# Values and denominators of a pair of steps in one column-tiled batch: 20 batches a group in place of 36

## The chip, the cores and the metric

One core of one Trainium2 chip runs the whole program in one launch. The metric is the device time of that launch in microseconds (us), lower is better. Durations come from one profiled execution; its own device time stands beside its span below.

## What is computed

One block of a language model over 2 x 2048 tokens of width 1024: an embedding of four-token contexts, layer norm, causal attention with 32 query heads over 8 key/value heads of width 32, its output projection, layer norm, and a last linear layer whose weight is corrected through a Fourier matrix. The change touches attention alone:

```
scores = jnp.einsum('bhqd,bhkd->bhqk', q, k) / math.sqrt(HEAD_DIM)
scores = jnp.where(causal[None, None, :, :], scores, jnp.float32(-1e+20))
attn = jax.nn.softmax(scores, axis=-1)
out = jnp.einsum('bhqk,bhkd->bhqd', attn, v)
```

## The kernel before

Three parts follow one another. `part_a` gathers the embeddings, normalises them and computes rotated queries, keys and values. `part_b` is attention. `part_c` is the output projection and the last layer. `part_b` takes most of the time and is all that changes.

**Groups and steps.** `part_b` runs 16 groups, each of one key/value head and its 4 query heads. A group has 36 steps (`STEPS`): for each of 8 query blocks `c` of 256 rows, first the diagonal block of 256 keys, then the `c` earlier ones. A step's work goes over four engines:

- PE computes the step's scores in two halves of 128 keys (`scores`, L1022). A half is two matmuls of 512 columns, into one of two slots of PSUM, `st_ps`. In a diagonal step each is followed by a small mask matmul (L1026). A half waits until the exponential of the same half of the step before has been taken (`exp_done`).
- ACT takes the exponential of each half (L878) into `probs`, which has 8 slots, one a step. Before it refills a slot it waits for PE and POOL to be done with it.
- POOL adds up the exponentials of a set of steps for the denominators (`set_sum`, L848 to L860). A set (`SETS`) is two steps, or the diagonal step alone where `c` is even: 16 pairs and 4 singles, 20 sets a group.
- PE multiplies by the values (`values`, L1040), three steps behind the scores (`LAG`), and with the last step of a set multiplies POOL's sum by ones (`denominators`, L1057, waits for `sum_done`). Both are column-tiled: the four heads are matmuls with 32 output columns each, which run side by side in the four quarters of the array. A step's values are 8 matmuls, which the profile shows as 16 records, the denominators 4, shown as 8. All else on PE uses the whole array.

**The maxima of the next rows.** Softmax needs each row's maximum before its scores. PE computes the scores of a later group once more in another layout (`row_scores`, L983, one matmul of 512 columns into one of three banks, `mx_ps`; the narrower blocks of the diagonal end with a mask matmul, L987), and DVE reduces each bank (L922). A bank is given again once DVE has reduced what it held (`max_done`). There are 140 such products and 4 transposes ("turn", L992) a group, four or five a step, 18 steps ahead of the scores (`LEAD`).

**The order of PE's work** is written out by hand in `group`: in each step two entries of the maxima, the two halves of the scores, two more entries (a fifth lies between the halves), then `batch(g, s - LAG)`.

Of the kernel before, what the change touches and what calls it, by code (L numbers as in the profile page):

```python
# [540 lines left out]
QW = CT // 2  # L541
# [11 lines left out]
LAG = 3  # L553
# [13 lines left out]

SETS = sum_sets()
SET_OF = [j for j, steps in enumerate(SETS) for s in steps]
LEAD, FIRST_LEAD = 18, 14  # L570
TURN_AFTER = 5
FOUR_AT, DELTA_AT = 8, 36
# [42 lines left out]
def part_b(nc, hand, w0_hi, w0_lo, q_hi, q_lo, k_hi, k_lo, v_dram, o_dram, den_dram, recip_dram, w_o_t, w_base_t,  # L615
           w1_dram, enc, fourier_t):

    with ExitStack() as ctx:
# [49 lines left out]
        def _(sp):  # L668
# [54 lines left out]
            def group(g, first, last):  # L723
                output_weight(g)
                first_reciprocals(g)

                def after_scores(s):
                    sp.wait_ge(st_ready, 2 * (g * NS + s + 1))

                def next_q(c):  # L730
                    if not last:
                        after_scores(LAST_OF_ROWS[c])
                        load_q(g + 1, c)
                    elif c < 2:
                        after_scores(LAST_OF_ROWS[c])
                        load_attended(sp, hand, o_dram, recip_dram, c)

                def next_k_max(c):
                    if not last:
                        sp.wait_ge(max_ready, g * NE + K_MAX_LAST[c] + 1)  # L740
                        load_k(k_max, g + 1, c, k_max_loaded)
                    elif c % 2 == 1:
                        sp.wait_ge(max_ready, g * NE + max(K_MAX_LAST[c - 1:c + 1]) + 1)
                        sp.dma_start(hand.w_in[c // 2][:], w1_dram[c // 2 * P:(c // 2 + 1) * P, :]
                                     ).then_inc(hand.w1_loaded[c // 2], 16)

                def next_k_score(c):
                    if not last:
                        after_scores(K_LAST[c])
                        load_k(k_score, g + 1, c, k_score_loaded)  # L750

                def next_v(c):
                    if not last:
                        sp.wait_ge(batch_done, g * NS + K_LAST[c] + 1)
                        load_v(g + 1, c)

                next_q(0)
                if not first:
                    store(g - 1, QH - 1)
                store(g, 0)  # L760
                send_rows(g, 2)
                next_k_max(0)
                store(g, 1)
                store(g, 2)
                next_q(1)
                next_k_max(1)
                store(g, 3)
                next_k_max(2)
                next_k_max(3)
                send_rows(g, 3)  # L770
                store(g, 4)
                next_q(2)
                if not last:
                    send_rows(g + 1, 0)
                store(g, 5)
                if not last:
                    send_rows(g + 1, 1)
                next_k_score(0)
                store(g, 6)
                next_k_score(1)  # L780
                next_v(0)
                next_k_score(2)
                next_v(1)
                next_q(3)
                next_k_score(3)
                next_v(2)
                next_v(3)

# [26 lines left out]
        @block.gpsimd  # L815
        def _(pool):
            nc.gpsimd.memset(k_score[M_ROW:P, :].bitcast(F32), 1.0).then_inc(k_ones_done, 1)
            pool.wait_ge(k_ones_done, 1)
            for c in range(DC):
                pool.wait_ge(base_in[c], 16)  # L820
                pool.wait_ge(delta_taken, c + 1)
                nc.gpsimd.tensor_tensor(hand.base[:, c, :], hand.base[:, c, :], hand.four[c][:], ALU.add
                                        ).then_inc(w1_ready, 1)

            for t in range(TPC):
                pool.wait_ge(hand.v_stored[t], 16 * CHUNKS)
            for s in range(2):
                pool.wait_ge(hand.rot_stored[s], 16 * CHUNKS * QK_TILES)
            step = Steps(pool, sum_step, 0)

            def probs_of(g, s, k, lo):
                return probs[:, (g * NS + s) % SLOTS, k, :, lo:QW]

            def exp_waited(g, s, k):
                pool.wait_ge(exp_done, 2 * (g * NS + s) + k + 1)

            def set_sum(g, j):

                q = g * len(SETS) + j
                at = sums[:, q % SUM_SLOTS]  # L840
                diagonal = [s for s in SETS[j] if STEPS[s][0] == STEPS[s][1]]
                wide = [(s, k) for s in SETS[j] for k in range(2) if k == 0 or s not in diagonal]
                if q >= SUM_SLOTS:
                    g_old, j_old = divmod(q - SUM_SLOTS, len(SETS))
                    pool.wait_ge(batch_done, g_old * NS + SETS[j_old][-1] + 1)
                if len(wide) == 1:
                    exp_waited(g, diagonal[0], 1)
                    nc.gpsimd.tensor_tensor(at[:, :, P:QW], probs_of(g, diagonal[0], 0, P),  # L848
                                            probs_of(g, diagonal[0], 1, P), ALU.add).then_inc(sum_done, 1)
                    return  # L850
                exp_waited(g, *wide[1])
                step.do(nc.gpsimd.tensor_tensor(at, probs_of(g, *wide[0], 0), probs_of(g, *wide[1], 0), ALU.add))  # L852
                exp_waited(g, *wide[2])
                step.do(nc.gpsimd.tensor_tensor(at, at, probs_of(g, *wide[2], 0), ALU.add))  # L854
                if diagonal:
                    lo, last = P, (diagonal[0], 1)
                else:
                    lo, last = 0, wide[3]
                exp_waited(g, *last)
                nc.gpsimd.tensor_tensor(at[:, :, lo:QW], at[:, :, lo:QW], probs_of(g, *last, lo), ALU.add  # L860
                                        ).then_inc(sum_done, 1)

            for g in range(GROUPS):
                for j in range(len(SETS)):
                    set_sum(g, j)

        @block.scalar
        def _(act):

            def exps(g, s, half):  # L870
                c, i = STEPS[s]
                n, lo = g * NS + s, P if i == c and half == 1 else 0
                act.wait_ge(st_ready, 2 * n + half + 1)
                if half == 0 and n >= SLOTS:
                    g_old, s_old = divmod(n - SLOTS, NS)
                    act.wait_ge(batch_done, n - SLOTS + 1)
                    act.wait_ge(sum_done, g_old * len(SETS) + SET_OF[s_old] + 1)
                nc.scalar.activation(probs[:, n % SLOTS, half, :, lo:QW], st_ps[:, half, :, lo:QW], ACT.Exp,  # L878
                                     scale=float(HD) ** -0.5).then_inc(exp_done, 1)

            def take(g, c):
                act.wait_ge(batch_done, g * NS + LAST_OF[c] + 1)
                if g * QH + c >= 2:
                    act.wait_ge(stored[c % 2], STORE * (g * (QH // 2) + c // 2))
                nc.scalar.copy(od_sb[:, c % 2], od_ps[:]).then_inc(od_copied, 1)  # L885
# [83 lines left out]
        def _(pe):  # L969
# [59 lines left out]
            def values(g, s):  # L1029
# [7 lines left out]
                for k in range(2):  # L1037
                    lo = P if i == c and k == 1 else 0
                    for h in range(GROUP):
                        mm = nc.tensor.matmul(od_ps[h * HD:(h + 1) * HD, 0, lo:QW], vs[:, 2 * i + k, :],  # L1040
                                              probs[:, n % SLOTS, k, h, lo:QW], start=s in FIRST_OF and k == 0,
                                              stop=False)
                return mm

            def denominators(g, s):

# [12 lines left out]
                return mm  # L1059

            def products(g, s):
                mm = values(g, s)
                if s == SETS[SET_OF[s]][-1]:
                    mm = denominators(g, s)
                mm.then_inc(batch_done, 1)

            def batch(g, s):
                if s >= 0:
                    products(g, s)
                elif g > 0:  # L1070
                    products(g - 1, s + NS)

            def group(g, first, last):
                for s in range(NS):
                    entries = entries_in(s, first, last)
                    ends = min(2, len(entries) // 2)
                    for more, n in entries[:ends]:
                        give(g + more, n)
                    scores(g, s, 0)
                    for more, n in entries[ends:len(entries) - ends]:  # L1080
                        give(g + more, n)
                    scores(g, s, 1)
                    for more, n in entries[len(entries) - ends:]:
                        give(g + more, n)
                    batch(g, s - LAG)

# [372 lines left out]
```

## Time and profile before

| | |
|---|---|
| median of 3 runs | 3505.76 us (3503.0 to 3506.37) |
| the profiled execution | 3505.48 us, span 3503.7 us |
| first to last column-tiled batch | 767 to 2752 us of the span |
| PE busy | 3364.4 us (96%) |
| DVE busy | 2239.2 us (64%) |
| ACT busy | 1420.5 us (41%) |
| POOL busy | 2265.2 us (65%) |
| TensorE clock granted | 0.982 of full speed |

PE is TensorE's matmul, PEld its weight load, which runs beside it. A matmul's record is longer than the distance to the next one's start, since they are pipelined. So what a matmul costs is read from start to start. "Idle before" names what ended the idle time of the engine.

### The profile page before, as it was taken

How to read it: one execution, taken by the hardware profiler on the slowest of the kernel's cores; microseconds unless marked ns; L12 is line 12 of the kernel's file. 1: busy time of each engine (PE TensorE's matmuls, PEld its weight loads, DVE VectorE, ACT ScalarE, POOL GpSimd, SP SyncE). 2: the span in 40 equal slices, each digit the busy share in tenths (PEclk: the TensorE clock that was granted, in tenths of full speed). 3: DMA queues.
4: the chain of work that ended last, by engine and by line, in shares of the span. 5: the costliest groups of instructions: out<-in, count | busy, mean ns of one | idle time of the engine just before them, and what ended most of it. 6: DMA issues, size and time to landing. Idle time of an engine off the chain costs nothing. (4 is left out here: it accounts for less than half of the span.)

```text
span 3503.7 us, 60330 instructions
## 1 busy us (share of the span) xinstructions
PE 3364.4 (96%) x24768; PEld 2343.2 (67%) x24768; DVE 2239.2 (64%) x3594; ACT 1420.5 (41%) x1677; POOL 2265.2 (65%) x1042
## 2 busy tenths in 40 slices
PE   1999999999999999999999999999999799999999
PEld 1778888646666666666666666666665488888887
DVE  3667777657777777777777777777774344444443
ACT  2222233125555555555555555555556300111100
POOL 3443320048999999999999999999999522333321
PEclk8999999969999999999999999999999899999999
DMA  8999984721221222122122112212212253344342
GB/s 231 245 255 232 234 226 127 193 101 41 65 61 34 63 63 56 38 66 58 40 68 60 41 49 64 51 39 67 55 39 52 85 99 94 91 95 93 87 95 67
DMA packets 248214, 334.52 MB, mean 95 GB/s; under 512 B 64346, under 2 KB 153818, under 8 KB 247938
## 3 DMA queue, kind: packets, MB, share of 16 engines
q1 hardware_dynamic: 229506, 263.54, 28.4%
q0 software_dynamic: 18432, 67.12, 9.0%
q8 instruction: 195, 3.19, 0.4%
q14 instruction: 81, 0.66, 0.1%
HBM read 227.80 MB, written 101.71 MB: 94 GB/s over the span
## 5 line engine op out<-in xcount | busy, mean ns | idle before, releaser
L922 DVE TENSOR_REDUCE mpart<-mx_ps 128x1 f32<-128x512 f32 (+3 forms) x2240 | 1407.3, 670 | 518.4 <-PE mx_ps L987 251.1
L878 ACT ACTIVATE probs<-st_ps 128x1024 f32<-128x1024 f32 (+1 forms) x1152 | 1063.0, 974 | 782.0 <-PE st_ps L1022 592.7
L983 PE MATMUL mx_ps<-k_max,qs 96*128 96x512 f32 (+3 forms) x2560 | 836.0, 410 | 4.3 <-PEq L158 2.6
L852 POOL TENSOR_TENSOR sums<-probs 128x1024 f32<-128x1024 f32 x256 | 610.3, 2384 | 119.7 <-ACT probs L878 119.7
L1022 PE MATMUL st_ps<-qs,k_score 98*128 98x512 f32 (+1 forms) x2304 | 676.9, 405 | 0.4
L854 POOL TENSOR_TENSOR sums<-sums,probs 128x1024 f32<-128x1024 f32 x256 | 614.4, 2400 | 20.6 <-ACT probs L878 0.6
L983 PEld LDWEIGHTS mx_ps<-k_max,qs 96*128 96x128 f32 x2560 | 444.3, 193 | 256.7 <-DVE mpart L922 148.2
L1040 PE MATMUL od_ps<-probs,vs 128*32 128x256 f32 (+1 forms) x9216 | 592.2, 375 | 0.4 <-ACT od_sb L885 0.4
L860 POOL TENSOR_TENSOR sums<-sums,probs 128x1024 f32<-128x1024 f32 (+1 forms) x256 | 539.3, 2107 | 20.5 <-ACT probs L878 0.5
L1022 PEld LDWEIGHTS st_ps<-qs,k_score 98*128 98x128 f32 x2304 | 431.2, 193 | 83.7 <-ACT probs L878 12.3
L1215 POOL TENSOR_TENSOR h<-h,bb 128x1024 f32<-128x1024 f32 x32 | 104.1, 3253 | 509.4 <-DVE xn_c L1289 509.4
L1040 PEld LDWEIGHTS od_ps<-probs,vs 128*32 128x32 f32 x9216 | 241.7, 109 | 259.0 <-issue 147.7
L291 POOL DMA_INDIRECT hbuf<-in_tok_table,idx_all x128 | 192.6, 1504 | 308.6 <-DMA hbuf<-in_tok_table,idx_all 168.3
L491 PE MATMUL qk_ps<-x_hi,w_hi 128*128 128x512 f32 x640 | 253.9, 397 | 18.3 <-ACT rotation L343 15.9
L491 PE MATMUL qk_ps<-x_lo,w_hi 128*128 128x512 f32 x640 | 251.0, 392 | 0.0
L491 PE MATMUL qk_ps<-x_hi,w_lo 128*128 128x512 f32 x640 | 251.0, 392 | 0.0
L1277 DVE TENSOR_TENSOR h<-oc_ps,h_in 128x1024 f32<-128x1024 f32 x31 | 38.0, 1224 | 256.3 <-PE oc_ps L1330 256.3
L1057 PE MATMUL od_ps<-sums,ones 128*32 128x256 f32 (+1 forms) x2560 | 184.5, 360 | 16.1 <-POOL sums L860 16.1
L987 PE MATMUL mx_ps<-masks 128*128 128x128 bf16 (+2 forms) x704 | 181.0, 257 | 0.0
L1242 ACT ACTIVATE std_c<-var_c 128x1 f32<-128x1 f32 x32 | 6.5, 203 | 404.2 <-DVE var_c L1284 404.2
L1330 PE MATMUL f_ps<-w_hi,xc_hi 128*128 128x512 f32 x512 | 158.6, 391 | 6.7 <-DVE xc_lo L1299 6.7
L1330 PE MATMUL oc_ps<-w_hi,a_hi 128*128 128x512 f32 x496 | 156.6, 397 | 7.5 <-DVE a_lo L1267 7.5
(108 smaller groups left out, 3950.1 us busy)
## 6 DMA issues: line engine op xcount, KB each, us to landing
qs<-q_hi_scratch SPq DMA_DIRECT2D x128, 256.0 KB, 4.8
h_scratch<-hbuf SPq DMA_DIRECT2D x32, 512.0 KB, 8.9
q_hi_scratch<-rot_hi SPq DMA_DIRECT2D x64, 256.0 KB, 4.1
q_lo_scratch<-rot_lo SPq DMA_DIRECT2D x64, 256.0 KB, 4.8
qs<-q_lo_scratch SPq DMA_DIRECT2D x64, 256.0 KB, 5.8
o_scratch<-od_sb SPq DMA_DIRECT2D x128, 128.0 KB
o_in<-o_scratch SPq DMA_DIRECT2D x32, 512.0 KB, 4.9
o_in<-recip_scratch SPq DMA_DIRECT2D x128, 128.0 KB, 7.9
```

The lines of the kernel that those rows point to most:

```text
L291: nc.gpsimd.indirect_dma_start(hbuf[:, m % 2, t, :], None, tables[k], bass.IndirectOffsetOnAxis(ap=idx[:, m, j:j + 1], axis=0), compute_op ...
L491: mm = nc.tensor.matmul(qk_ps[:, f % 2, :], w[a], x[b], start=(c == 0 and k == 0), stop=(c == DC - 1 and k == 2))
L852: step.do(nc.gpsimd.tensor_tensor(at, probs_of(g, *wide[0], 0), probs_of(g, *wide[1], 0), ALU.add))
L854: step.do(nc.gpsimd.tensor_tensor(at, at, probs_of(g, *wide[2], 0), ALU.add))
L860: nc.gpsimd.tensor_tensor(at[:, :, lo:QW], at[:, :, lo:QW], probs_of(g, *last, lo), ALU.add).then_inc(sum_done, 1)
L878: nc.scalar.activation(probs[:, n % SLOTS, half, :, lo:QW], st_ps[:, half, :, lo:QW], ACT.Exp, scale=float(HD) ** -0.5).then_inc(exp_done, 1)
L922: nc.vector.tensor_reduce(mpart[:, rows, kc], scored, AX, ALU.max).then_inc(max_done, 1)
L983: mm = nc.tensor.matmul(out[:, j], qs[c][0:K_ROWS, h, t * P:(t + 1) * P], k_max[0:K_ROWS, kc * CT:kc * CT + w], start=j == 0, stop=not dia ...
L1022: mm = nc.tensor.matmul(out[:, :, lo:QW], k_score[0:M_ROW + 2, kt * P:(kt + 1) * P], qs[c // 2][0:M_ROW + 2, h:h + 2, at + lo:at + QW], st ...
L1040: mm = nc.tensor.matmul(od_ps[h * HD:(h + 1) * HD, 0, lo:QW], vs[:, 2 * i + k, :], probs[:, n % SLOTS, k, h, lo:QW], start=s in FIRST_OF a ...
L1057: mm = nc.tensor.matmul(od_ps[h * HD:(h + 1) * HD, 1, lo:QW], ones[:], sums[:, q % SUM_SLOTS, h, lo:QW], start=False, stop=s in LAST_OF)
L1330: mm = nc.tensor.matmul(into[:, n * 512:(n + 1) * 512], x[a][:, c, :], (w_hi, w_lo)[b][l][:, c, n * 512:(n + 1) * 512], start=(c == 0 and ...
```

## The change

Values of a pair's first step are no longer computed alone, a step earlier. Once a set's last step is due, the values of all its steps follow one another and the denominators come behind them. `batch_done` counts sets, not steps, and every wait on it (SP's loads of values, POOL's sums, ACT's exponentials and copies) is rewritten to the count of the set. ACT's own wait for `sum_done` falls, as the set's batch contains it. Of the entries of the maxima, two still stand next to a batch, but only one at the end of a step where no batch stands; the rest go between the halves.

```diff
+BATCH_STEPS = [steps[-1] for steps in SETS]
...
-                    act.wait_ge(batch_done, n - SLOTS + 1)
-                    act.wait_ge(sum_done, g_old * len(SETS) + SET_OF[s_old] + 1)
+                    act.wait_ge(batch_done, g_old * len(SETS) + SET_OF[s_old] + 1)
...
             def products(g, s):
-                mm = values(g, s)
-                if s == SETS[SET_OF[s]][-1]:
-                    mm = denominators(g, s)
-                mm.then_inc(batch_done, 1)
+
+                steps = SETS[SET_OF[s]]
+                if s == steps[-1]:
+                    for k in steps:
+                        values(g, k)
+                    denominators(g, s).then_inc(batch_done, 1)
...
+            def batch_behind(s):
+                return (s - LAG) % NS in BATCH_STEPS
+
             def group(g, first, last):
                 for s in range(NS):
                     entries = entries_in(s, first, last)
-                    ends = min(2, len(entries) // 2)
-                    for more, n in entries[:ends]:
+                    head = min(2 if batch_behind(s - 1) else 1, len(entries) // 2)
+                    tail = len(entries) - min(2 if batch_behind(s) else 1, len(entries) // 2)
+                    for more, n in entries[:head]:
                         give(g + more, n)
                     scores(g, s, 0)
-                    for more, n in entries[ends:len(entries) - ends]:
+                    for more, n in entries[head:tail]:
                         give(g + more, n)
                     scores(g, s, 1)
-                    for more, n in entries[len(entries) - ends:]:
+                    for more, n in entries[tail:]:
                         give(g + more, n)
                     batch(g, s - LAG)
```

On DVE, ACT and POOL the instructions keep their order. On PE they move. Two neighbouring steps late in a group, with products of 512 columns as their only entries, stood so before (mx_ps are products of the maxima, st_ps scores, od_ps the column-tiled batch):

```order
L983 MATMUL mx_ps<-k_max,qs 128x512 [waits max_done] x2
L1022 MATMUL st_ps<-qs,k_score 128x512 [waits exp_done]
L1022 MATMUL st_ps<-qs,k_score 128x512
L1022 MATMUL st_ps<-qs,k_score 128x512 [waits exp_done]
L1022 MATMUL st_ps<-qs,k_score 128x512
L983 MATMUL mx_ps<-k_max,qs 128x512 [waits max_done] x2
L1040 MATMUL od_ps<-probs,vs 32x256 x8
L983 MATMUL mx_ps<-k_max,qs 128x512 [waits max_done] x2
L1022 MATMUL st_ps<-qs,k_score 128x512 [waits exp_done]
L1022 MATMUL st_ps<-qs,k_score 128x512
L1022 MATMUL st_ps<-qs,k_score 128x512 [waits exp_done]
L1022 MATMUL st_ps<-qs,k_score 128x512
```

And now, from one batch to the two products ahead of the next:

```order
L982 MATMUL mx_ps<-k_max,qs 128x512 [waits max_done] x2
L1021 MATMUL st_ps<-qs,k_score 128x512 [waits exp_done]
L1021 MATMUL st_ps<-qs,k_score 128x512
L982 MATMUL mx_ps<-k_max,qs 128x512 [waits max_done]
L1021 MATMUL st_ps<-qs,k_score 128x512 [waits exp_done]
L1021 MATMUL st_ps<-qs,k_score 128x512
L982 MATMUL mx_ps<-k_max,qs 128x512 [waits max_done] x2
L1021 MATMUL st_ps<-qs,k_score 128x512 [waits exp_done]
L1021 MATMUL st_ps<-qs,k_score 128x512
L982 MATMUL mx_ps<-k_max,qs 128x512 [waits max_done]
L1021 MATMUL st_ps<-qs,k_score 128x512 [waits exp_done]
L1021 MATMUL st_ps<-qs,k_score 128x512
```

The batch between the two steps is gone, and of the four products that stood on its two sides two remain between the last half of the one step and the first of the next; the others went between the halves.

The batch that ends the second step was this:

```order
L983 MATMUL mx_ps<-k_max,qs 128x512 [waits max_done] x2
L1040 MATMUL od_ps<-probs,vs 32x256 x8
L1057 MATMUL od_ps<-sums,ones 32x256 [waits sum_done]
L1057 MATMUL od_ps<-sums,ones 32x256 x3
L983 MATMUL mx_ps<-k_max,qs 128x512 [waits max_done] x2
```

It is now this:

```order
L982 MATMUL mx_ps<-k_max,qs 128x512 [waits max_done] x2
L1039 MATMUL od_ps<-probs,vs 32x256 x16
L1054 MATMUL od_ps<-sums,ones 32x256 [waits sum_done]
L1054 MATMUL od_ps<-sums,ones 32x256 x3
L982 MATMUL mx_ps<-k_max,qs 128x512 [waits max_done] x2
```

The eight matmuls of the first step's values joined the second's; the wait for POOL's sum stands behind all sixteen.

## Rows read from the trace of the kernel before

**Rows 1.** The page: busy tenths in 40 slices of the span.

```profile
PE   1999999999999999999999999999999799999999
...
POOL 3443320048999999999999999999999522333321
```

**Rows 2.** Windows, 767 to 2752 us; columns: stretch, its length, busy us per engine.

```profile
767.00:2752.00 1985.00, 1966.56 (x18285) 1207.41 (x18284) 1418.67 (x2376) 1139.23 (x1290) 1829.34 (x828) 1.00 0.21 52
```

**Rows 3.** Timeline of PE, 1605 to 1610 us; start, us, engine, operation.

```profile
1605.49 1.07 PE L1040 MATMUL od_ps<-probs,vs 128*32 128x256 f32 x16
1606.38 0.61 PE L1057 MATMUL od_ps<-sums,ones 128*32 128x256 f32 x8
1606.92 0.72 PE L983 MATMUL mx_ps<-k_max,qs 96*128 96x512 f32 x2
1607.49 1.07 PE L1022 MATMUL st_ps<-qs,k_score 98*128 98x512 f32 x4
1608.40 0.63 PE L983 MATMUL mx_ps<-k_max,qs 96*128 96x512 f32 x2
1608.96 1.07 PE L1040 MATMUL od_ps<-probs,vs 128*32 128x256 f32 x16
1609.96 0.50 PE L983 MATMUL mx_ps<-k_max,qs 96*128 96x512 f32 x1
```

**Rows 4.** Timeline of all engines, 1613.7 to 1620.6 us.

```profile
1616.81 2.68 DVE L922 TENSOR_REDUCE mpart<-mx_ps 128x1 f32<-128x512 f32 x4 [0.16 <-PE mx_ps L983]
1616.84 1.09 PE L1022 MATMUL st_ps<-qs,k_score 98*128 98x512 f32 x4
1617.51 1.94 ACT L878 ACTIVATE probs<-st_ps 128x1024 f32<-128x1024 f32 x2 [0.90 <-PE st_ps L1022]
```

**Rows 5.** Timeline of all engines, 2695.9 to 2697.4 us (last group, no maxima left).

```profile
2695.56 1.02 ACT L878 ACTIVATE probs<-st_ps 128x1024 f32<-128x1024 f32 x1
...
2696.00 1.37 PE L1022 MATMUL st_ps<-qs,k_score 98*128 98x512 f32 x4
2696.63 0.30 PEld L1022 LDWEIGHTS st_ps<-qs,k_score 98*128 98x128 f32 x2 [0.34 <-ACT probs L878]
...
2697.29 0.42 PE L1040 MATMUL od_ps<-probs,vs 128*32 128x256 f32 x4
```

**Rows 6.** Timeline of all engines, 799.5 to 801.5 us (first group).

```profile
799.18 2.48 DVE L922 TENSOR_REDUCE mpart<-mx_ps 128x1 f32<-128x512 f32 x4 [0.81 <-PE mx_ps L983]
...
800.53 0.19 PEld L983 LDWEIGHTS mx_ps<-k_max,qs 96*128 96x128 f32 x1 [0.41 <-DVE mpart L922]
```

**Rows 7.** Timeline of PE, 1507 to 1512 us: products with a mask behind them.

```profile
1507.77 0.42 PE L983 MATMUL mx_ps<-k_max,qs 96*128 96x384 f32 x1
...
1508.07 0.42 PE L983 MATMUL mx_ps<-k_max,qs 96*128 96x384 f32 x1
...
1510.26 0.47 PE L983 MATMUL mx_ps<-k_max,qs 96*128 96x512 f32 x1
...
1510.61 0.48 PE L1022 MATMUL st_ps<-qs,k_score 98*128 98x512 f32 x1
```

**Rows 8.** Waits of PE, 767 to 2640 us: total us, times, longest.

```profile
PE mx_ps L983 <- DVE mpart L922: 0.5, 1, 0.5
```

**Rows 9.** Waits of PE, 2640 to 2752 us.

```profile
PE od_ps L1057 <- POOL sums L860: 16.1, 8, 3.6
```

**Rows 10.** Groups by line, whole span: busy us, mean ns | idle us before.

```profile
L854 POOL TENSOR_TENSOR sums<-sums,probs 128x1024 f32<-128x1024 f32 x256 | 614.4, 2400 | 20.6 <-ACT probs L878 0.6
L852 POOL TENSOR_TENSOR sums<-probs 128x1024 f32<-128x1024 f32 x256 | 610.3, 2384 | 119.7 <-ACT probs L878 119.7
...
L860 POOL TENSOR_TENSOR sums<-sums,probs 128x1024 f32<-128x1024 f32 (+1 forms) x256 | 539.3, 2107 | 20.5 <-ACT probs L878 0.5
...
L848 POOL TENSOR_TENSOR sums<-probs 128x512 f32<-128x512 f32 x64 | 82.2, 1285 | 2.3 <-ACT probs L878 2.3
```

**Rows 11.** Waits of POOL, 1637 to 1762 us (one group).

```profile
POOL sums L852 <- ACT probs L878: 6.6, 5, 2.0
```

More of the change, by code:

```diff
@@ L753, in next_v @@
                     if not last:
-                        sp.wait_ge(batch_done, g * NS + K_LAST[c] + 1)
+                        sp.wait_ge(batch_done, g * len(SETS) + SET_OF[K_LAST[c]] + 1)
                         load_v(g + 1, c)
@@ L843, in set_sum @@
                 if q >= SUM_SLOTS:
-                    g_old, j_old = divmod(q - SUM_SLOTS, len(SETS))
-                    pool.wait_ge(batch_done, g_old * NS + SETS[j_old][-1] + 1)
+                    pool.wait_ge(batch_done, q - SUM_SLOTS + 1)
                 if len(wide) == 1:
@@ L881, in take @@
             def take(g, c):
-                act.wait_ge(batch_done, g * NS + LAST_OF[c] + 1)
+                act.wait_ge(batch_done, g * len(SETS) + SET_OF[LAST_OF[c]] + 1)
                 if g * QH + c >= 2:
@@ L1039, in values @@
                     for h in range(GROUP):
[L1040 to L1043, printed above, removed]
+                        nc.tensor.matmul(od_ps[h * HD:(h + 1) * HD, 0, lo:QW], vs[:, 2 * i + k, :],
+                                         probs[:, n % SLOTS, k, h, lo:QW], start=s in FIRST_OF and k == 0, stop=False)
             def denominators(g, s):
```

## The prediction

> **What bounds the kernel now.** First the page's slices: PE is at nine tenths or more in nearly every slice, and from the eleventh slice to the thirtieth POOL is as full [rows 1]. Then the window of the column-tiled batches, 767 to 2752 us: 1985 us, 124.1 a group, in which PE is busy 1966.6, POOL 1829.3, DVE 1418.7 and ACT 1139.2 [rows 2]. The waits of PE say which of them ends its idle time: before 2640 us it waited 0.5 us for DVE, once [rows 8]; behind that, at the end of the last group, 16.1 us for POOL [rows 9]. So PE's own sequence sets the time of 15 groups, and what is to be learnt is in its timeline, from start to start.
>
> **What a batch costs beyond its matmuls.** Four score matmuls take 0.91 us (1607.49 to 1608.40), 0.23 each, 0.46 a half; a product of the maxima has the same 512 columns, so 0.23. Two products ahead of a batch take 0.56 us (1608.40 to 1608.96) and not 0.46: 0.10 for going in. The values of a step take 0.89 us with denominators behind them (1605.49 to 1606.38), and 1.00 with a product behind them (1608.96 to 1609.96): 0.11 for coming out. The two products after a batch take 0.57 us (1606.92 to 1607.49): 0.11 more [rows 3]. Together 0.32; as the joined values also spare the slower start of a batch's first four records, I take 0.33. The bounds are 0.32 and 0.36 by the hundredths to which the starts are given.
>
> **What is removed.** 36 batches a group become 20. That is 16 fewer, 256 in all, each worth 0.33 us. No matmul is removed. Ten of the 256 lie after the last group's eighteenth step, where no maxima are left and PE waits for POOL [rows 9]; there a shorter PE gives nothing. 246 x 0.33 = **81 us** off.
>
> **What takes the removed batch's place.** A batch did more than cost: while PE was in it, ACT took exponentials and DVE reduced banks. In a step without a batch PE now comes back too soon. Take the two steps whose new order is shown above, all products 512 columns wide, and count from the start of the first half, S0. Up to the S0 of the next step lie two halves and three products: 2 x 0.46 + 3 x 0.23 = 1.62 us. But that S0 needs the exponential of this one. ACT starts 0.67 us after S0 does (1616.84 to 1617.51), one exponential takes 1.02, both 1.94 [rows 4, 5]. PE goes on 0.05 us after the end (2695.56 + 1.02 = 2696.58; the weight load that waited starts at 2696.63), and the load that waited is no longer hidden: two score matmuls take 0.66 us to the batch at 2697.29, where two products take 0.56 [rows 3, 5], 0.10 to 0.11 more. So S0 comes effectively at 0.67 + 1.02 + 0.05 + 0.11 = 1.85 us: **0.23 late**. The second half likewise: due at 1.85 + 0.46 + 0.23 = 2.54, possible at 0.67 + 1.94 + 0.05 + 0.11 = 2.77: 0.23 more. Such a pair loses 0.45 where it saves 0.33.
>
> I went through the 16 pairs by the entries that lie in each gap. A mask behind a product lengthens it: 0.30 us at 384 columns (1507.77 to 1508.07), 0.35 at 512 (1510.26 to 1510.61) [rows 7], and this fills the gap. The group's steps at which no batch stands are these:
> - 4, 7, 11, 29, 31, 33: only wide products, as above. 6 x 0.45 = 2.7 us.
> - 9 and 27: the next step is diagonal, its own masks delay its second half, so only the first wait stays, 0.23 each.
> - 16: two masked products and, in step 17, none but a transpose: 0.22 + 0.34 = 0.56.
> - 18, 20, 25: a gap of 1.74 to 1.88 us, with the waits for the second half: 0.13, 0.10, 0.19.
> - 1, 14, 35: masked products and a diagonal step, over 1.85 us: nothing.
>
> In 22 and 27 there is a turn as a fifth entry, and there the banks bind. DVE reduces one every 0.60 us ((2.48 - 0.68) / 3) when it is never idle, and PE's load waits for it [rows 6]. Eight or nine entries between batches are 4.8 to 5.4 us of DVE, which stands idle through the longer batch. I put 0.45 on step 22 in all and 0.19 more on 27.
>
> The sum is 2.7 + 0.46 + 0.56 + 0.42 + 0.45 + 0.19 = 4.8 us a group, 72 in 15 groups. The last group's first six such steps add 2, its other ones nothing: **74 us** on.
>
> **What costs nothing.** POOL's order stays, and it needs 1846 us for its sums plus 41 between the parts of a set, 118.0 a group [rows 10], against PE's 124.1 - 5.3 + 4.8 = 123.6. In a group it now waits 6.6 us for exponentials [rows 11], so the sums are ready as before; the denominators follow the second step's values as before. ACT's waits for a slot look eight steps back, the joined batch comes four steps later at most. SP's loads of values are asked for one step later, and are needed five steps after that. If POOL's cover went, PE would wait in front of the denominators.
>
> **The sum.** 3505.5 us of the profiled execution, which is 0.3 below the median of the runs, - 81 + 74 = **3498 us**.
>
> **A rule against one term.** In rows 5 the load stands idle until ACT's exponential has ended, and costs 0.11 after it. The Trainium skill (TensorE: Matmul & The Clock Gate, "Architectural detail: the array is 16x 32x32, not 1x 128x128") says that TensorE's queue is a partial reorder window that can pull a weight load ahead of matmuls in flight. By that rule the load could be done while its matmul waits; this trace disagrees wherever PE waits. It is rival B.
>
> **Rivals.**
> - A, the waits don't come: ACT and DVE keep up. For it: ACT is busy 57% of the window and DVE 71% [rows 2], and no wait for either is there now. Against it: 1.62 against 1.74 without any load. It would take 81 us off; a group would be 118.8 us of PE, just above POOL's 118.0, so hardly less is left: 3425 us.
> - B, waits come, the load of the waiting matmul is ready. For it: a load elsewhere runs under the matmul ahead. Against it: rows 5 and 6. Some 20 waits a group, 0.11 less each, 15 groups: 33 us less, 3465.
> - C, **slower**: the other ten pairs don't get off lightly. I let them lose 2.1 us together; the group breaks even at 5.3 - 2.7 = 2.6. Their gaps lie at 1.74 to 1.88 us against 1.85, so a few hundredths of a us each decide, or one more late bank. For it: DVE now idles before a step's four reductions [rows 4], but with the batches joined it has eight to start in the 3.9 us between two of them (8 x 0.23 + 4 x 0.46 + 0.10 + 0.11) and can catch up only three in the batch. If they lose 3.7 together, the group is 1.0 us longer: 3520. If all 16 lose 0.45, 1.9 longer: 3534.
> - That the change doesn't do what it says can be left out: the new order of PE is shown above.
>
> **How the numbers follow.** My case 0.62, A 0.08, B 0.10, C 0.20. My case's own range, 3485 to 3511, is the ten lighter pairs off by 0.9 us a group either way (0.9 x 15 = 13). About 0.2%, 7 us, is what a measurement of this kernel can tell from none, and the forecast lies on that bound. Faster by more: A, B and 0.25 of mine, 0.43. Within: 0.33 of mine and 0.02 of C. Slower: 0.18 of C and 0.04 of mine, 0.22. The range reaches from B to C's first value, 3464 to 3520, and leaves out A and the end of C.
>
> **What would show it.** Batches: 320 starts in place of 576, a joined one 0.89 + 0.86 + 0.54 = 2.3 us long. The waits of PE, now empty, should name ACT's probs in front of st_ps, 12 and more times a group, with the score matmul starting 0.05 us after an exponential's end and 0.34 us (0.23 + 0.11) to the next. A group should be 123.5 us from POOL's first sum to the next. No such waits and groups of 119 us mean A. Waits with only 0.23 us to the next matmul mean B. Waits for DVE's mpart in most pairs, or waits in steps 1, 14 and 35, mean C. A saving per batch far from 0.33 would make all of it wrong.

## The result, and the profile after

| | before | changed |
|---|---|---|
| median, measured side by side | 3504.38 us (3502.95 to 3506.37) | 3606.32 us (3600.94 to 3613.07) |
| the profiled execution | 3505.48 us, span 3503.7 | 3600.94 us, span 3599.1 |
| PE busy | 3364.4 us | 3392.0 us |
| TensorE clock granted, mean | 0.982 | 0.971 |

The changed kernel takes 1.0291 times as long, 95% interval 1.0279 to 1.0304. That is 102 us slower than before, 108 above the forecast and 86 above the range.

The slices that [rows 1] shows of before, and the clock (tenths of full speed), from the page of the changed kernel:

```profile
PE   2999999999999999999999999999999799999999
...
POOL 3443220169888988988988988888898722222222
PEclk8999999879999999999999999999999899999999
```

The slices are too coarse: PE still looks full. POOL, which [rows 1] had at nine tenths from the eleventh slice to the thirtieth, drops to eight in most of them. The largest of PE's waits in the same stretch as [rows 8], 767 to 2640 us (total us, times, longest):

```profile
PE mx_ps L982 <- DMA qs<-q_lo_scratch: 54.8, 14, 4.5
```

This is one stall a group, and it names neither ACT nor DVE (the two rows behind it, both DVE, come to 7.5 us). It names a DMA, the load of the next group's queries. It lies in the third step of the group. Timeline of PE in the changed kernel, 1541 to 1554 us:

```profile
1542.53 0.70 PE L1021 MATMUL st_ps<-qs,k_score 98*128 98x512 f32 x2
1547.44 0.77 PE L982 MATMUL mx_ps<-k_max,qs 96*128 96x512 f32 x1 [4.21 <-DMA qs<-q_lo_scratch]
1548.01 1.05 PE L1021 MATMUL st_ps<-qs,k_score 98*128 98x512 f32 x2
1548.86 1.05 PE L982 MATMUL mx_ps<-k_max,qs 96*128 96x512 f32 x2
1549.85 2.77 PE L1039 MATMUL od_ps<-probs,vs 128*32 128x256 f32 x32
1552.45 0.60 PE L1054 MATMUL od_ps<-sums,ones 128*32 128x256 f32 x8
```

Before 1542.53 all is as forecast; after 1547.44 everything is slow: two products in 0.99 us, not 0.56, and the values of two steps in 2.60 us, not 1.75. The windows around it say why (stretch, length, busy us of PE, PEld, DVE, ACT, POOL, then granted clock, share of the DMA engines, GB/s):

```profile
1536.00:1543.00 7.00, 7.00 (x70) 4.29 (x69) 4.29 (x8) 3.02 (x4) 6.84 (x4) 1.00 0.29 46
1543.00:1547.40 4.40, 0.23 (x2) 0.00 (x0) 0.89 (x3) 1.02 (x1) 3.51 (x2) 0.70 0.72 171
1547.40:1551.00 3.60, 3.56 (x17) 2.09 (x21) 1.98 (x3) 1.02 (x1) 0.74 (x1) 0.50 0.00 0
1551.00:1558.00 7.00, 7.00 (x83) 4.32 (x76) 3.84 (x8) 2.78 (x5) 4.17 (x3) 0.96 0.48 132
```

PE stands idle for 4.2 us here; the clock is at 0.50, the 1.2 GHz level, when it starts again, and in the 3.6 us after. The Trainium skill (TensorE: Matmul & The Clock Gate, "What's actually happening") gives half rate as the state of an idle array, and the trace agrees. A stall is thus dearer than its idle time: its step takes 10.9 us from start to start (median of groups 2 to 14), where in run 1 below, without the stall, it takes 4.7. That is 6.2 us a group, of which 3.9 stand in the list of waits (54.8 / 14).

**Why the queries came late.** SP's queue tells. SP in the changed kernel, 1530 to 1560 us (SPq are DMAs as SP issues them):

```profile
1532.42 0.38 SPq L679 DMA_DIRECT2D vs<-v_scratch  x1
...
1539.69 0.38 SPq L679 DMA_DIRECT2D vs<-v_scratch  x1
1540.12 0.98 SPq L89 DMA_DIRECT2D qs<-q_hi_scratch  x2
1541.14 0.43 SPq L89 DMA_DIRECT2D qs<-q_lo_scratch  x1
```

SP in the kernel before, the same group, 1502 to 1530 us:

```profile
1506.01 0.38 SPq L678 DMA_DIRECT2D vs<-v_scratch  x1
1506.44 2.02 SPq L89 DMA_DIRECT2D qs<-q_hi_scratch  x2
1508.51 0.43 SPq L89 DMA_DIRECT2D qs<-q_lo_scratch  x1
```

SP issues in program order: `next_v(0)`, `next_k_score(2)`, `next_v(1)`, `next_q(3)`, `next_k_score(3)`. `next_v(1)` waits for the batch that last reads those values, that of step 32. It was a batch of its own; joined with step 33's it ends one step later, in the next group's first step. Behind it stands `next_q(3)`, the queries of the next group's last row block, whose product is due in the third step. The first scores of that group and the product that reads the queries stood so before, in PE's timeline from 1502 to 1520 us:

```profile
1506.56 0.48 PE L1022 MATMUL st_ps<-qs,k_score 98*128 98x512 f32 x1
...
1514.20 0.47 PE L983 MATMUL mx_ps<-k_max,qs 96*128 96x512 f32 x1
```

And the first scores in the changed kernel, in PE's timeline from 1530 to 1560 us:

```profile
1535.05 0.47 PE L1021 MATMUL st_ps<-qs,k_score 98*128 98x512 f32 x1
```

So the last query load is issued 1.95 us behind the first scores before and 6.09 behind them after: 4.14 later. In this group it had nothing to spare: the product started 5.7 us after the issue, and the view of the tile `qs` before gives these landings:

```profile
DMA to landing us min/median/max: 4.8/5.1/5.6
```

This group is one of the tighter ones. In ten of the fourteen groups from the second to the fifteenth the load was issued 0.90 us behind the first scores before, 5.2 us earlier than in the changed kernel, and in nine of these ten it had 0.2 to 1.1 us to spare.

The list of waits of [rows 8] had a second row, which I did not take up:

```profile
PE mx_ps L983 <- DMA qs<-q_lo_scratch: 0.2, 1, 0.2
```

So my theory was: **SP's order costs some 6.2 x 15 = 93 us, and the joining itself next to nothing, on the wrong side.** The rival was that the joined batches cost more than forecast and the stall merely shows where. The rest of the changed profile is as forecast: a joined batch with its denominators is 2.3 us long, and ACT's exponentials now hold PE's weight loads, about 13 times a group.

### The profile page after: what moved, and what is told of

It reads as the page before. It is cut to its first block and busy times, and to the rows that moved or that the text cites. A ratio compares the mean times of both kernels' runs of the same rounds, so it can differ in the third digit from the quotient of the medians.

```text
span 3599.1 us, 60331 instructions
## 1 busy us (share of the span) xinstructions
PE 3392.0 (94%) x24768; PEld 2358.3 (66%) x24768; DVE 2222.6 (62%) x3594; ACT 1415.6 (39%) x1677; POOL 2265.2 (63%) x1042
## 5 line engine op out<-in xcount | busy, mean ns | idle before, releaser
L921 DVE TENSOR_REDUCE mpart<-mx_ps 128x1 f32<-128x512 f32 (+3 forms) x2240 | 1384.8, 669 | 621.3 <-PE mx_ps L982 388.4
L982 PE MATMUL mx_ps<-k_max,qs 96*128 96x512 f32 (+3 forms) x2560 | 859.5, 406 | 66.6 <-DMA qs<-q_lo_scratch 58.9
L1021 PE MATMUL st_ps<-qs,k_score 98*128 98x512 f32 (+1 forms) x2304 | 788.8, 423 | 7.1 <-ACT probs L877 6.2
L852 POOL TENSOR_TENSOR sums<-probs 128x1024 f32<-128x1024 f32 x256 | 609.8, 2382 | 136.8 <-ACT probs L877 136.8
L982 PEld LDWEIGHTS mx_ps<-k_max,qs 96*128 96x128 f32 x2560 | 461.2, 195 | 299.5 <-issue 180.4
L1039 PE MATMUL od_ps<-probs,vs 128*32 128x256 f32 (+1 forms) x9216 | 555.6, 380 | 1.0 <-ACT od_sb L884 1.0
L1021 PEld LDWEIGHTS st_ps<-qs,k_score 98*128 98x128 f32 x2304 | 410.6, 194 | 128.3 <-ACT probs L877 74.0
L1039 PEld LDWEIGHTS od_ps<-probs,vs 128*32 128x32 f32 x9216 | 269.9, 112 | 239.8 <-issue 110.0
L884 ACT COPY od_sb<-od_ps 128x512 f32<-128x512 f32 x128 | 75.0, 586 | 233.4 <-PE od_ps L1054 227.7
```

The costliest lines, as they stand in the source:

```text
L921: nc.vector.tensor_reduce(mpart[:, rows, kc], scored, AX, ALU.max).then_inc(max_done, 1)
L982: mm = nc.tensor.matmul(out[:, j], qs[c][0:K_ROWS, h, t * P:(t + 1) * P], k_max[0:K_ROWS, kc * CT:kc * CT + w], start=j == 0, stop=not dia ...
L1021: mm = nc.tensor.matmul(out[:, :, lo:QW], k_score[0:M_ROW + 2, kt * P:(kt + 1) * P], qs[c // 2][0:M_ROW + 2, h:h + 2, at + lo:at + QW], st ...
```

## The experiments

A "pair" below is the time from the start of the step whose batch fell to the start of the step after the next, in PE's timeline, as the median over groups 2 to 13. A pair's balance is this less its time before.

### 1. The queries ahead of the values

```diff
-                next_v(1)
                 next_q(3)
                 next_k_score(3)
+                next_v(1)
```

> The changed kernel, but on SP the loads of the next group's last queries and of its last keys stand ahead of the load of values that waits for batch (32, 33). Theory Q (the queries' load is queued behind a wait that the change moved past the end of the group): the 4.4 us wait of PE for qs in step 2 goes, and with it the half clock behind it, 6.2 us a group over 15 groups, 93 us of the 102: 3512 us. Rival M (the time went into many small waits, and the long one only stands where they gather): under 60 us come back, over 3545. Either way the pairs of wide products keep their 0.10 to 0.12 us over the kernel before.

Measured: 3508.30 us (3504.1 to 3512.4) beside 3503.53, ratio 1.0015 [1.0006, 1.0025]. Of the 102 us the order of two loads gives 98 back. The stall is gone; PE's waits from 767 to 2640 us are

```profile
PE mx_ps L991 <- DVE mcol L924: 6.0, 15, 0.4
PE mx_ps L982 <- DVE mpart L921: 1.5, 6, 0.5
```

Freed of the stall, the joining by itself can be read: 4.8 us slower than before, where my sum had it 7.5 faster. POOL's first sums of two groups lie 124.5 us apart (median); before 123.84. The first row is new too: once a group PE stands 0.4 us in front of a turn. It belongs to the pair in steps 16 and 17, and the table below comes back to it.

### 2. The late wait alone, without the joining

```diff
-                        sp.wait_ge(batch_done, g * NS + K_LAST[c] + 1)
+                        sp.wait_ge(batch_done, g * NS + K_LAST[c] + (2 if c == 1 else 1))
```

> The kernel before with one number changed: SP's load of the second quarter of the values waits for the batch after the one it needs, the one at the end of the next group's first step, as in the changed kernel. Nothing on PE, DVE, ACT or POOL moves. Theory Q: PE waits some 4 us for qs in step 2 of 15 groups and then runs at half clock for some us, 5 to 6 us a group: 3580 to 3600 us. Rival M: the queue can bear one batch of delay, below 3525.

Measured: 3592.02 us, ratio 1.0255 [1.0237, 1.0273], 88.5 us slower. The waits of PE, 767 to 2640 us:

```profile
PE mx_ps L983 <- DMA qs<-q_lo_scratch: 51.7, 14, 4.3
```

One wait that is satisfied a step later, in a kernel otherwise as before, makes nearly the whole loss. This and the first run settle it from both sides.

### 3. The products placed as before

```diff
-                    head = min(2 if batch_behind(s - 1) else 1, len(entries) // 2)
-                    tail = len(entries) - min(2 if batch_behind(s) else 1, len(entries) // 2)
+                    head = min(2, len(entries) // 2)
+                    tail = len(entries) - min(2, len(entries) // 2)
```

> As the run with the queries first, but with two entries of the maxima at both ends of every step, as before the change. If the exponentials alone set the pair (1.85 us from half to half), the time stays: four products in the gap fill 1.84 us, the second half still loses 0.47, within 5 us of that run. If the three banks bind (the fourth product in a row waits for the third reduction before it, 0.57 us late by my count), 0.1 us in each of six wide pairs and more in masked ones, 15 to 40 us slower than that run.

Measured: 3581.77 us, 1.0221 [1.0192, 1.0250], 73 us over the first run, far more than expected. The wide pairs are only 0.12 us worse (6.80 against 6.68). The banks are what bind: with four products in a row where a batch fell, DVE's reductions come too late. PE's waits, 767 to 2700 us:

```profile
PE mx_ps L982 <- DVE mpart L921: 60.4, 172, 1.6
```

The loss is unevenly spread. A group in which DVE does not compute `w_lo` (L948, the low part of an output weight) takes 127.5 us, 3.4 more than in the first run: that is the banks, some 50 us in 15 groups. In the eight groups with `w_lo` step 15 takes 6.77 us, and twice 8.26, where it took 5.64; in the others it takes 4.98, less than its 5.28. What makes the step long in those eight is DVE's subtraction, which takes 2.6 us there in place of 1.0, for the reason told in the last section. So the change's new placing is worth 73 us with the batches joined; I had the sign, not the size: the expectation put 15 to 40 us on the banks and nothing on this subtraction.

### 4. Exponentials of half the columns

This kernel leaves out the exponential of half of each step's new columns, so that ACT is early. The rest is the first run's.

```diff
+                hi = QW if n < 2 * SLOTS else (lo + QW) // 2
-                nc.scalar.activation(probs[:, n % SLOTS, half, :, lo:QW], st_ps[:, half, :, lo:QW], ACT.Exp,
+                nc.scalar.activation(probs[:, n % SLOTS, half, :, lo:hi], st_ps[:, half, :, lo:hi], ACT.Exp,
```

> As the run with the queries first, but from the seventeenth step on each exponential covers only half of its columns; what it leaves out keeps older values. ACT's time for one falls from 1.02 to about 0.59 us, PE's work is the same. If the waits for exponentials take the 0.45 us a pair, they go: 246 batches at 0.33 less some 0.6 us a group for the banks, 3433 us. If something else holds PE in the steps without a batch (the banks of the maxima, the weight loads), less than 30 us is gained over that run. If a removed batch is worth much less than 0.33, it stays over 3460 with no wait for ACT.

Measured: 3478.66 us, 0.9928 [0.9910, 0.9946]: 30 us less than the first run, not the 75 expected. A wide pair went from 6.68 to 6.40 us, while without any wait it would be about 6.24. PE's weight loads in 767 to 2700 us show what came next:

```profile
PEld mx_ps L982 <- DVE mpart L921: 168.0, 413, 1.8
```
```profile
PEld mx_ps L983 <- DVE mpart L922: 92.9, 329, 0.8
```

The first row is experiment 3's, the second this one's. The exponentials were the later of two limits that lie close together; beneath them the banks hold.

### 5. Maxima over half the columns

The reductions read half of their bank, so that DVE is early; the maxima leave out the other half. All else is the first run's.

```diff
-                nc.vector.tensor_reduce(mpart[:, rows, kc], scored, AX, ALU.max).then_inc(max_done, 1)
+                nc.vector.tensor_reduce(mpart[:, rows, kc], scored[:, :, 0:w // 2], AX, ALU.max).then_inc(max_done, 1)
```

> Queries first with DVE's reductions over half of their columns, the exponentials whole. If the exponentials hold PE in the wide pairs and the banks only stand behind them, a wide pair stays at its 0.11 to 0.15 us over the kernel before, and only the pairs with a turn and masked ones (14, 16, 22, 27) gain, at most 1 us a group: 3490 to 3508 us. If the banks are what holds PE, it comes near the run with short exponentials, 3479, or below.

Measured: 3485.11 us, 0.9958 [0.9943, 0.9973], 5 us below the span expected. Weight loads that waited, 767 to 2640 us: first the kernel of run 1, then this one.

```profile
PEld st_ps L1021 <- ACT probs L877: 61.2, 190, 0.4
PEld mx_ps L982 <- DVE mpart L921: 54.5, 221, 0.8
```
```profile
PEld st_ps L1021 <- ACT probs L877: 80.1, 210, 0.4
...
PEld mx_ps L982 <- DVE mpart L921: 0.9, 2, 0.5
```

The waits for banks are gone, those for exponentials grew, and the wide pairs stayed at 6.68 us (1.75 + 4.93). What was gained, 1.06 us a group, came in the steps with turns and masked products. That is 15 of the 23 us; in the profiled executions another 7 came in the first group, where more products of the maxima fall in a step (133.1 us in the first run, 126.1 here).

### 6. Both halved

Experiments 4 and 5 together: half of the exponentials' columns and half of the maxima's are left out. Against run 1:

```diff
+                hi = QW if n < 2 * SLOTS else (lo + QW) // 2
-                nc.scalar.activation(probs[:, n % SLOTS, half, :, lo:QW], st_ps[:, half, :, lo:QW], ACT.Exp,
+                nc.scalar.activation(probs[:, n % SLOTS, half, :, lo:hi], st_ps[:, half, :, lo:hi], ACT.Exp,
...
-                nc.vector.tensor_reduce(mpart[:, rows, kc], scored, AX, ALU.max).then_inc(max_done, 1)
+                nc.vector.tensor_reduce(mpart[:, rows, kc], scored[:, :, 0:w // 2], AX, ALU.max).then_inc(max_done, 1)
```

> As the run with the short exponentials, and DVE's reductions too cover half of their columns. PE's work is the same. The run with short exponentials stayed 45 us above what the removed batches should have left. Theory D (the banks of the maxima hold PE once ACT no longer does): the rest goes, until POOL's sums bind, 118.0 us a group: 3425 to 3440 us, with PE waiting for POOL. Rival S (a removed batch is worth less than 0.33): it stays over 3460.

Measured: 3433.40 us, 0.9806 [0.9791, 0.9821], 75 us under run 1. A wide pair takes 1.64 + 4.60 = 6.24 us, which is its time before less 0.29. This is the batch's own price, seen where no wait fills the gap. The weight loads waited for a bank 10 times:

```profile
PEld mx_ps L983 <- DVE mpart L922: 6.8, 10, 0.7
```

Alone, the one limit's removal gave 30 us, the other's 23; both gave 75. Two limits so close must be taken away together. Not all waits are gone: the turn in step 17 still waits 0.35 us for DVE, and a group with `w_lo` takes 120.4 us, one without 119.6.

### 7. One product at each end of a joined pair's steps

```diff
-                    head = min(2 if batch_behind(s - 1) else 1, len(entries) // 2)
-                    tail = len(entries) - min(2 if batch_behind(s) else 1, len(entries) // 2)
+                    head = min(2 if batch_behind(s - 1) and batch_behind(s) else 1, len(entries) // 2)
+                    tail = len(entries) - min(2 if batch_behind(s - 1) and batch_behind(s) else 1, len(entries) // 2)
```

> Queries first, all pairs joined, but one entry of the maxima at each end of a joined pair's steps too, so that four products and not three lie between the first halves (1.85 us, what an exponential needs) and six up to the second. By my recurrence the exponentials no longer hold PE and only the banks do, once, in front of the sixth product: a wide pair is 0.08 us shorter than with the queries first, 3500 us, give or take 5. If the banks suffer more from a start of one product after the batch, it is slower than that run.

Measured: 3510.24 us, 1.0021 [1.0011, 1.0032]: a miss. The wide pairs in 7, 29, 31 and 33 gained 0.06 (6.62 against 6.68), where 0.08 was expected, but the two pairs with a turn lost more: that of steps 22 and 23 took 7.51 against 6.89, of which 0.23 is a product that had stood ahead of the pair's start and now stands inside it, and that of 27 and 28 took 7.66 against 7.32. Pair 20 lost 0.2 as well. With a fifth entry between the halves the reductions came too thick: the waits of weight loads for a bank rose from 54.5 to 116.9 us.

### 8. Five pairs joined, eleven left as before

By run 1 only five sets gain in every group, those whose first batch stood in PE's steps 18, 20, 25, 35 and 1: -0.18, -0.18, -0.11, -0.30 and -0.30 us, 1.07 a group together. They are the steps (15, 16), (17, 18), (22, 23), (32, 33) and (34, 35). This kernel joins these alone, with SP's order of run 1.

```diff
-BATCH_STEPS = [steps[-1] for steps in SETS]
+JOINED = (15, 17, 22, 32, 34)
+BATCH_STEPS = [s for steps in SETS for s in steps if s == steps[-1] or steps[0] not in JOINED]
...
-                if s == steps[-1]:
+                if steps[0] not in JOINED:
+                    values(g, s)
+                elif s == steps[-1]:
                     for k in steps:
                         values(g, k)
+                if s == steps[-1]:
                     denominators(g, s).then_inc(batch_done, 1)
```

> Queries first, and only five of the group's 16 pairs joined, those that came out shorter than before by step in the run with the queries first (steps 1, 35: 0.30 us each, 18 and 20: 0.18, 25: 0.11), the other eleven with two batches and two entries at both ends as before. If a pair's balance is its own (a batch saved against the waits in its gap), the five sum to 1.07 us a group, 17 us in 16 groups: 3487 us. If the balance moves from pair to pair (the backlog of DVE and POOL carries over), less than half of it, over 3495.

Measured: **3483.30 us** (3479.3 to 3486.2) beside 3501.95, ratio 0.9948 [0.9935, 0.9962]. It beats both kernels, the one before by 18.7 us. The group is 122.7 us, 1.14 less than before. The weight loads waited for banks less than in [rows 8]'s stretch of before (136.8 us there, 387 times) and for exponentials exactly as before:

```profile
PEld mx_ps L983 <- DVE mpart L922: 117.8, 334, 0.8
PEld st_ps L1022 <- ACT probs L878: 6.2, 15, 0.4
```

### 9. SP's new order in the kernel before

```diff
-                next_v(1)
                 next_q(3)
                 next_k_score(3)
+                next_v(1)
```

> The kernel before with SP's new order alone (queries and last keys ahead of the second load of values), all 36 batches kept. If the five joined pairs made the gain of their run, this is the kernel before, within 3 us. If part of that gain came from the earlier loads, it is faster by more than 5 us.

Measured: 3499.96 us beside 3503.65, 0.9993 [0.9982, 1.0004], no difference that these runs can tell; by the interval the order gains 6 us at most. So the gain of experiment 8, 18.7 us, comes from the joining and not from the order.

### 10. Five pairs joined, with SP's old order

Against experiment 8:

```diff
+                next_v(1)
                 next_q(3)
                 next_k_score(3)
-                next_v(1)
```

> The five joined pairs with SP's order as it was. Pair (32, 33) is joined, so the queries stand behind a batch that ends after the next group's first step: theory Q gives the stall back in full, 5.9 to 6.2 us in 15 groups, 3483 + 90 = 3573 us. A queue that needs more than this one pair to fall behind would leave it under 3500.

Measured: 3591.36 us, 1.0252 [1.0232, 1.0272]; the waits of PE, 767 to 2640 us:

```profile
PE mx_ps L983 <- DMA qs<-q_lo_scratch: 57.7, 14, 4.4
```

The order is worth 108 us here, 18 more than expected: the step with the stall takes 11.7 us from start to start, not 10.9. Of the five joined sets it is (32, 33) for whose batch `next_v(1)` waits.

### 11. A sixth pair

Run 1 gave the pair in steps 14 and 15 a balance of -0.33 us in the groups in which DVE does not also compute `w_lo` (L948) there. This kernel joins it as well and moves that subtraction a step forward.

```diff
-JOINED = (15, 17, 22, 32, 34)
+JOINED = (11, 15, 17, 22, 32, 34)
...
-                    if 0 <= g - W_O_GROUP < DC and s in (12, 14):
-                        weight_low(g - W_O_GROUP, (12, 14).index(s))
+                    if 0 <= g - W_O_GROUP < DC and s in (12, 13):
+                        weight_low(g - W_O_GROUP, (12, 13).index(s))
```

> The five joined pairs and pair (11, 12) as a sixth, with DVE's second subtraction of the output weight moved from behind step 14 to behind step 13. In the run with the queries first this pair came out 0.33 us shorter in the groups without that subtraction and 0.03 longer in the eight with it. If the subtraction in a joined pair was what cost there, all groups gain: 0.33 x 15, 5 us under the run with five, 3478 us. If the place does not matter, 3482 or above.

Measured: 3484.46 us, 0.9948 [0.9930, 0.9965], the same as with five. Without the subtraction the pair takes 7.34 us, 0.33 less than before, as expected; in the eight groups with it, 8.45. Why is told in the last section.

## Why the prediction was wrong

**The step that failed** stands under "What costs nothing": "SP's loads of values are asked for one step later, and are needed five steps after that." True of the values, and not the question. The prediction named what waits, and not what is queued behind it on SP: the queries of the last row block. They had from nothing to 1.1 us to spare, and the changed kernel asked for them 4.1 to 5.2 us later. Runs 1 and 2 show what that was: 98 us back by the order of two loads, 88.5 us on by one wait. None of the three rivals had it; C was slower, but for another reason.

**The joining itself** was forecast at -7.5 us and measured at +4.8. By terms:

| pair, by its first step | balance forecast, us | measured (run 1) |
|---|---|---|
| 4, 7, 11, 29, 31, 33 | +0.12 each | +0.09 to +0.15 |
| 9 | -0.10 | -0.02 |
| 14 | -0.33 | -0.33; +0.03 with `w_lo` |
| 16 | +0.23 | +0.50 |
| 18, 20, 25 | -0.20, -0.23, -0.14 | -0.18, -0.18, -0.11 |
| 22 | +0.12 | +0.09 |
| 27 | +0.09 | +0.33 |
| 1, 35 | -0.33 each | -0.30 each |

- **What is removed**: 0.33 us a batch was 0.30 in the pairs 1 and 35, which meet no wait, and 0.29 in the wide pairs of run 6. In the table this shows in the pairs 1, 18, 20, 25 and 35, 0.16 us a group together, some 2 us of the 12 by which the joining was off.
- **What takes its place**: right in mechanism and, for the wide pairs, in size. They are six of the sixteen. Timeline of PE in run 1, where one is forecast at 1.85 us from S0 to S0:

```profile
1615.74 0.63 PE L1021 MATMUL st_ps<-qs,k_score 98*128 98x512 f32 x2
1616.21 0.40 PE L982 MATMUL mx_ps<-k_max,qs 96*128 96x512 f32 x1
1616.45 0.63 PE L1021 MATMUL st_ps<-qs,k_score 98*128 98x512 f32 x2
1616.91 0.64 PE L982 MATMUL mx_ps<-k_max,qs 96*128 96x512 f32 x2
1617.49 0.73 PE L1021 MATMUL st_ps<-qs,k_score 98*128 98x512 f32 x2
1618.06 0.40 PE L982 MATMUL mx_ps<-k_max,qs 96*128 96x512 f32 x1
1618.41 0.73 PE L1021 MATMUL st_ps<-qs,k_score 98*128 98x512 f32 x2
1618.98 0.63 PE L982 MATMUL mx_ps<-k_max,qs 96*128 96x512 f32 x2
1619.54 1.72 PE L1039 MATMUL od_ps<-probs,vs 128*32 128x256 f32 x32
```

  The next S0 starts 1.75 us after this one, and as its weight load waited, it lasts 0.57 (1617.49 to 1618.06) where this one lasts 0.47: 0.10 to 0.11 more, 1.86 by the forecast's count of 1.85. The second half starts at 1618.41, and takes 0.57 again. The batch comes at 1619.54, 2.05 after S0. So rival B, a ready load, is false. In groups 2 to 15 of this run 168 halves without a mask had a load that waited for an exponential. Each load started 0.04 us after the exponential's end, and each of these halves takes 0.56 to 0.58 us, where the median of the others is 0.47.
- **The pairs 9, 16 and 27** were off by 0.08, 0.27 and 0.24 us, some 9 us in 15 groups, each for another reason. In 27 it is rival C's mechanism, a late bank: behind the turn a weight load waits 0.4 us, and with short maxima (experiment 5) the second step falls from 5.50 to 5.08 us. In 16 it is the turn itself, in step 17. It waits 0.40 us for DVE to reduce the last product and take the column maxima (`mcol`), which a batch used to cover; with short maxima it waits 0.16, and the pair falls from 6.93 to 6.70. In 9 it is an exponential: the forecast had the masks cover the second half's wait, but that half's load starts 0.05 us after the exponential's end; short maxima leave the pair at 6.57, short exponentials bring it to 6.30.
- **The pair 14** was forecast as meeting nothing. In the eight groups with `w_lo` one subtraction, 1.04 us as before, stands between DVE's reductions here. The batch had covered it; now a weight load in step 15 waits 0.29 us for a bank, and the pair takes 7.7 us and not 7.34, some 3 us in all. The terms named so far come to 14 us, of the 12 measured.
- **Rival A** is answered by experiments 4 to 6: only with both ACT and DVE out of the way does the joined kernel come near A's 3425 us, at 3433.4. `w_lo` is 0.8 us in each of eight groups of what is left.
- **POOL's cover** held: PE waited for its sums 9.8 us in the whole changed kernel, less than the 16.1 of [rows 9].

The mean of such terms hides the useful fact in them: five pairs gained 1.07 us a group and the others gave it back. Experiment 8 took the five.

## What to carry to other kernels

A batch that is joined reports later. Follow every wait that is renumbered to its queue, SP's too, and ask of what stands behind it, not only of what waits, when it is needed and how much it has to spare; a row of 0.2 us in the list of waits already names a queue at its limit. A saved switch pays only where the gap that it leaves is filled by other work, so cost it place by place, and join only the places that gain.

## What the runs showed of the hardware

`w_lo`, one subtraction on DVE whose operands and result all lie in SBUF, takes from 0.71 to 2.67 us (2.67 in experiment 3), by where POOL's running sums stand. There are 16 of them, two a group in eight groups. By lines (busy us, mean ns), in the kernel before, then in experiment 6 and in experiment 11:

```profile
L949 DVE TENSOR_TENSOR w_lo<-w_raw,w_hi 128x512 fp32r<-128x512 f32 x16 | 14.1, 881 | 0.0
```
```profile
L949 DVE TENSOR_TENSOR w_lo<-w_raw,w_hi 128x512 fp32r<-128x512 f32 x16 | 36.3, 2267 | 0.0
```
```profile
L949 DVE TENSOR_TENSOR w_lo<-w_raw,w_hi 128x512 fp32r<-128x512 f32 x16 | 25.9, 1617 | 0.0
```

The timeline of experiment 6, 1517.8 to 1521 us, shows one of them:

```profile
1517.25 2.39 POOL L852 TENSOR_TENSOR sums<-probs 128x1024 f32<-128x1024 f32 x1
...
1518.21 1.97 DVE L949 TENSOR_TENSOR w_lo<-w_raw,w_hi 128x512 fp32r<-128x512 f32 x1
...
1519.71 2.70 POOL L854 TENSOR_TENSOR sums<-sums,probs 128x1024 f32<-128x1024 f32 x1
...
1520.51 0.45 PE L983 MATMUL mx_ps<-k_max,qs 96*128 96x384 f32 x1 [0.61 <-DVE mpart L922]
```

POOL's sum ends at 1519.64 and DVE's subtraction at 1520.18, 0.54 us later; it had been running since 1518.21. The sum that POOL began meanwhile takes 2.70 us, not the 2.38 of others. PE then waits 0.61 us for the reduction behind the subtraction. In both kernels and all eleven runs every one of the 16 subtractions ends 0.55 or 0.56 us after the sum of POOL that was running when it began; it takes 0.71 us where that sum had 0.17 us left. So the two do not share, they take turns. The Trainium skill (SBUF — State Buffer, "🔬 SBUF: two separate sides") has this as an exclusive lock between a DVE operation with two inputs in SBUF and a GpSimd operation that reads SBUF; the trace agrees. In experiment 11 the subtraction of the joined pair started 0.41 us behind the start of POOL's sum and took 2.51 us: this ate the gain of the sixth pair. A version that places it for the 0.71 us and joins six was not tried.

A second surprise was told above: 3.9 us of idle time on PE cost 6.2 a group. In the group shown the granted clock was 0.50, the 1.2 GHz level, in the 3.6 us after the stall, and from 1547.44 to the next step (1553.56) PE took 6.1 us for what takes 4.1 in run 1.
